# The expert layer joins the attention block: weights split on GpSimd beside the last heads, its layer norm by sequences, ranks made two tiles ahead

## The reference, cut to what matters

```python
x = x + _L0_attn_ref(_layernorm(x, axis=-1), ...)
x = x + _L0_ffn_ref(_layernorm(x, axis=-1), ...)
x = x + _L1_attn_ref(_layernorm(x, axis=-1), ...)     # 32 heads of 16, causal, ALiBi
x = x + _L1_ffn_ref(_layernorm(x, axis=-1), ...)      # below

scores = xf @ Wr.T                                    # 64 experts
top_vals, top_idx = jax.lax.top_k(scores, 16)
gates = jax.nn.softmax(top_vals, axis=-1)
G = zeros((N, 64)); G[n, top_idx] = gates
h = jnp.einsum('nd,krd->nkr', xf, A)                  # "ranks": 64 experts of rank 16
out = jnp.einsum('nkr,kdr->nd', h * G[:, :, None], B) * 2
```

## Time and profile before

| | us |
|---|---|
| median of 3 runs | 1530.74 (1530.06 to 1533.52) |
| the profiled execution, its own time | 1526.56 |
| its span, first to last instruction | 1524.8 |
| PE busy in the span | 1440.9 (94%) |
| DVE, ACT, POOL busy | 1020.6, 857.6, 537.7 |

### The profile page before, as it was taken

One profiled execution on the slowest core, in us unless ns is written; L12 is line 12 of the kernel. 1 busy time (PEld: TensorE's weight loads), 2 busy tenths in 40 slices (PEclk: granted clock), 3 DMA queues, 4 the chain that ended last, 5 costly groups with the idle time before them and its releaser, 6 DMA issues. The chain is left out here.

```text
span 1524.8 us, 25454 instructions
## 1 busy us (share of the span) xinstructions
PE 1440.9 (94%) x7696; PEld 1197.1 (79%) x7696; DVE 1020.6 (67%) x2549; ACT 857.6 (56%) x2184; POOL 537.7 (35%) x467
## 2 busy tenths in 40 slices
PE   6999999999999999999979999998799999985898
PEld 4788888888888888888867888887677777763687
DVE  7776667666677666776645333354788888997543
ACT  2766556665566655666543333212798989993110
POOL 5574465644656446563220000023433222101500
PEclk9999999999999999999999999999999999997999
DMA  5010010101101011000021111106445444403000
GB/s 169 10 47 15 28 43 21 34 14 27 41 21 34 14 27 41 21 14 8 8 84 42 63 61 42 55 0 110 98 77 105 77 103 78 84 1 114 8 21 28
DMA packets 37517, 71.98 MB, mean 47 GB/s; under 512 B 4992, under 2 KB 5376, under 8 KB 36864
## 3 DMA queue, kind: packets, MB, share of 16 engines
q1 hardware_dynamic: 29664, 55.35, 11.5%
q0 software_dynamic: 7776, 15.73, 7.2%
HBM read 60.58 MB, written 10.49 MB: 47 GB/s over the span
## 5 line engine op out<-in xcount | busy, mean ns | idle before, releaser
L822 ACT ACTIVATE a_probs<-a_probs,a_least 128x512 f32<-128x512 f32 (+3 forms) x256 | 143.0, 560 | 162.4 <-DVE a_least L683 157.7
L405 POOL TENSOR_TENSOR a_rotated<-a_by_cos,a_by_sin 128x512 f32<-128x512 f32 x80 | 103.7, 1296 | 223.8 <-DVE a_by_sin L706 221.7
L691 DVE TENSOR_TENSOR a_probsT_lo<-ps_out,a_probsT_hi 128x512 fp32r<-128x512 f32 (+3 forms) x256 | 118.6, 484 | 67.2 <-ACT a_probsT_hi L830 66.0
L830 ACT CAST a_probsT_hi<-ps_out 128x512 fp32r<-128x512 f32 (+3 forms) x256 | 101.5, 427 | 91.3 <-PE ps_out L556 90.5
L1774 ACT ACTIVATE a_probs<-a_probs,a_least 128x128 f32<-128x128 f32 (+3 forms) x256 | 142.1, 560 | 3.6 <-issue 1.8
L1658 DVE CUSTOM_DVE_ANT_0 a_probs<-ps_gate,a_causal 128x128 f32<-128x128 f32 (+3 forms) x256 | 117.1, 486 | 29.5 <-PE ps_gate L1508 19.4
L882 ACT ACTIVATE a_probs<-a_probs,a_inverse 128x128 f32<-128x128 f32 (+3 forms) x256 | 123.1, 553 | 9.6 <-DVE a_inverse L724 8.6
L64 PE MATMUL ps_up<-a_wo_hi,a_attended_hi 128*128 128x512 f32 x280 | 114.7, 410 | 6.6 <-DVE a_attended_lo L1738 1.7
L415 POOL TENSOR_TENSOR a_query_lo<-a_rotated,a_query_hi 128x512 fp32r<-128x512 f32 x64 | 82.6, 1291 | 107.6 <-ACT a_query_hi L842 107.6
L683 DVE CUSTOM_DVE_ANT_0 a_probs<-ps_out,a_causal 128x512 f32<-128x512 f32 (+2 forms) x192 | 101.1, 552 | 28.2 <-PE ps_out L66 28.1
L1666 DVE TENSOR_TENSOR a_probsT_lo<-ps_out,a_probsT_hi 128x384 fp32r<-128x384 f32 (+1 forms) x192 | 108.9, 596 | 2.6 <-ACT a_probsT_hi L1783 2.4
(11 more groups left out here) (271 smaller groups left out, 4083.3 us busy)
## 6 DMA issues: line engine op xcount, KB each, us to landing
a_raw<-in_wq SPq DMA_DIRECT2D x36, 256.0 KB, 2.7
a_raw<-in_wo SPq DMA_DIRECT2D x36, 256.0 KB, 2.7
a_stacked_q<-a_spill_q POOLq DMA_DIRECT2D x48, 128.0 KB, 4.6
a_stacked_k<-a_spill_k POOLq DMA_DIRECT2D x24, 256.0 KB, 4.3
f_raw<-in_gate SPq DMA_DIRECT2D x14, 256.0 KB, 2.8
f_raw<-in_up SPq DMA_DIRECT2D x14, 256.0 KB, 3.0
f_raw<-in_down SPq DMA_DIRECT2D x14, 256.0 KB, 3.6
a_raw<-in_wk SPq DMA_DIRECT2D x12, 256.0 KB, 2.8
```

Of the source, the lines that this page charges most:

```text
L405: nc.gpsimd.tensor_tensor(rotated[:], by_cos[:], by_sin[:], ALU.add).then_inc(rotation_added, 1)
L691: nc.vector.tensor_tensor(probsT[1][:, t % 2, 0:w], ps_turn[:, t % 2, 0:w], probsT[0][:, t % 2, 0:w].bitcast(F32), ALU.subtract).then_inc( ...
L822: nc.scalar.activation(tile, tile, ACT.Exp, bias=least[:, slot, i:i + 1], scale=-1.0, accum_out=total[:, slot, i:i + 1]).then_inc(exp_done, 1)
L830: nc.scalar.copy(probsT[0][:, t % 2, 0:w], ps_turn[:, t % 2, 0:w]).then_inc(turned_hi, 1)
```

## The change

`moe_phase` and its barrier are gone; a class `Moe` places the expert layer's tiles in memory that attention has done with, and the engines go on from the last head into it in the same block.

- **SP and GpSimd.** SP issues the loads of `down` and the router as soon as the last chunk's operands are out of their buffers. GpSimd splits them (18 instructions) behind its last attention piece, and then `up` (16 instructions) once all scores are made. ACT and DVE no longer split weights.
- **The order of the last outputs.** Tiles 0 and 1 are made in step 11 of the last chunk, tile 2 in step 12, tile 3 in step 13, and nothing in step 14. DVE takes each tile's moments right after adding it, and the layer norm of sequence 0 starts behind the last head. Tiles 4 to 7 are made later, between the router scores and the ranks of tile 0, in four different banks.
- **The layer norm by sequences.** Sequence 0 (tiles 0 to 3) comes first; sequence 1 follows between `rank(2)` and `rank(3)`. The router scores are made for half of the tokens at a time.
- **Ranks two tiles ahead.** PE's order is `turn(t + 1)`, `rank(t + 3)`, `make_out(t)`, so that what a tile's output needs is made one round before it. Outputs 5 and 7 have a bank of their own.

```diff
-SIDE1 = {0: "keys", 2: "values", 3: "spread", 4: "out", 6: "query"}
-BACK1 = (3, 5, 6)
+SIDE1 = {0: "keys", 2: "values", 3: "spread", 6: "query"}
+OUTS1 = {3: [(0, "back")], 4: [(1, "side")], 5: [(2, "back")], 6: [(3, "back")]}
+LAST_OUTS1 = {11: [(0, "back"), (1, "side")], 12: [(2, "side")], 13: [(3, "back")]}
...
     @block.sync
...
+        sp.wait_ge(query_out, 2 * 16 * 2 * CHUNKS1)
+        sp.wait_ge(keys_out, 2 * 16 * 2 * CHUNKS1)
+        moe.fetch_down(sp, (0, 1))
+        sp.wait_ge(side_made, side_count(CHUNKS1 - 1, 2))
+        moe.fetch_down(sp, (2, 3))
+        moe.sync(sp)
...
     @block.gpsimd
...
+        pool.wait_ge(score_made, 4 * (UNITS1 - HPC))
+        moe.split_first(pool)
+        pool.wait_ge(piece_split, piece_count(CHUNKS1 - 1, "wo"))
+        pool.wait_ge(score_made, 4 * UNITS1)
+        moe.split_up(pool)
...
     @block.tensor
...
+        moe.norm.turn(pe, 0)
+        turn_gathered(*last, *last)
+        moe.norm.ready(pe, 0)
+        pe.wait_ge(attend_read, UNITS1)
+        moe.make_scores(pe, 0)
+        turn_result(2 * CHUNKS1 - 1)
+        moe.rank(pe, 0, (0, 1))
+        moe.turn_scores(pe, 0)
+        for t in range(3):
+            make_last_out(t)
+        moe.rank(pe, 0, (2, 3))
+        make_last_out(3)
+        moe.tensor(pe)
...
     @block.vector
...
-                if last_steps:
+                if last_outs:
                     dve.wait_ge(read, count)
                     take_moments(nc, dve, m, 3, t)
...
+            if isinstance(c, int) and (c, s) == (CHUNKS1 - 1, STEPS1 - 2):
+                moe.norm.shift(dve, 0)
...
+        moe.norm.invert(dve, 0)
+        for t in range(QT):
+            moe.norm.normalise(dve, t)
+        for t in range(QT):
+            moe.norm.split(dve, t)
+        divide(*last)
+        split_attended(2 * CHUNKS1 - 1, CHUNKS1)
+        moe.pick(dve, 0)
+        for t in range(3):
+            add_last_out(t)
+        moe.gate_ranks(dve, 0)
+        add_last_out(3)
+        moe.vector(dve)
```

The new class, cut to the order of its work (its `pick`, `gate_ranks`, `turn` and `make_out` compute what those of `moe_phase` did; `pick` reads scores that ACT has copied out of PSUM for four tiles at once):

```diff
+    def split_first(self, pool):
...
+        def split(number, src, hi, lo, zero):
+            nc.gpsimd.tensor_tensor(hi, src, zero, ALU.add).then_inc(self.weights_hi, 1)
+            pool.wait_ge(self.weights_hi, number + 1)
+            nc.gpsimd.tensor_tensor(lo, src, hi.bitcast(F32), ALU.subtract).then_inc(self.weights_split, 1)
...
+    def sync(self, sp):
...
+        for i in range(2):
+            sp.wait_ge(self.weights_split, 4 * i + 5)
+            sp.dma_start(self.up_raw[i][:], m.dram["up1"][:, 4 * i:4 * i + 4, :]).then_inc(self.up_in[i], 16)
...
+    def tensor(self, pe):
+        every = range(DC)
+        self.rank(pe, 1, every)
+        self.turn(pe, 0)
+        self.rank(pe, 2, every)
+        pe.wait_ge(self.turned_split, 2)
+        self.norm.turn(pe, 1)
+        self.rank(pe, 3, every)
+        self.norm.ready(pe, 1)
+        self.turn(pe, 1)
+        self.make_out(pe, 0)
+        self.make_scores(pe, 1)
+        self.turn(pe, 2)
+        self.rank(pe, 4, every)
+        self.turn_scores(pe, 1)
+        self.make_out(pe, 1)
+        for t in range(2, NT):
+            if t + 1 < NT:
+                self.turn(pe, t + 1)
+            if t + 3 < NT:
+                self.rank(pe, t + 3, every)
+            self.make_out(pe, t)
...
+    def vector(self, dve):
+        norm = self.norm
+        norm.shift(dve, 1)
+        self.pick(dve, 1)
+        norm.invert(dve, 1)
+        for t in range(QT, NT):
+            norm.normalise(dve, t)
+        self.split_turned(dve, 0)
+        self.gate_ranks(dve, 1)
+        for t in range(QT, NT):
+            norm.split(dve, t)
+        self.pick(dve, 2)
+        self.gate_ranks(dve, 2)
```

More of the change, by code:

```diff
@@ L1219, in ffn0_attention1_phase, with outs @@
     result_turned, attended_split = sem("result_turned"), sem("attended_split")
-    def out_there(c, s):
-        return not isinstance(c, int) or (1 <= c if s < 8 else 0 <= c < CHUNKS1)
+    last_made, last_added = sem("last_made"), sem("last_added")
+    last = (CHUNKS1 - 1, STEPS1 - 1)
+    moe = Moe(nc, m, ctx, base, ffn, zeros, out)
+    def outs(c, s):
+        if not isinstance(c, int):
+            return OUTS1.get(s % 8, [])
+        if c == CHUNKS1 - 1 and s >= 8:
+            return LAST_OUTS1.get(s, [])
+        return OUTS1.get(s % 8, []) if (1 <= c if s < 8 else 0 <= c) else []
     def side(c, s):
@@ L1229, in side, with outs_until @@
             return what
[L1230 to L1240, removed]
+        return what if (c < CHUNKS1 - 1 if what == "query" or s >= 8 else 0 <= c < CHUNKS1) else None
     def steps_until(c, s):
-        steps = [(-1, k) for k in range(6, STEPS1)] + [(d, k) for d in range(CHUNKS1 + 1) for k in range(8 if d == CHUNKS1 else STEPS1)]
+        steps = [(-1, k) for k in range(6, STEPS1)] + [(d, k) for d in range(CHUNKS1) for k in range(STEPS1)]
         return [x for x in steps if x <= (c, s)]
+    def outs_until(c, s, bank):
+        return len([x for step in steps_until(c, s) for x in outs(*step) if x[1] == bank])
     def side_count(c, s):
@@ L1255, in back_count, with out_count @@
             return 6 * (c - 1) + back_count(1, s)
-        return len([x for x in steps_until(c, s) if back(*x)])
+        return outs_until(c, s, "back")
+    def out_count(c, s, at):
+        bank = outs(c, s)[at][1]
+        count = back_count(c, s) if bank == "back" else side_count(c, s)
+        return count - len([x for x in outs(c, s)[at + 1:] if x[1] == bank])
     def half_made(c, s):
@@ L1598, in step @@
                 norm.ready(pe, 1)
-            if s % 8 in (3, 4, 5, 6) and out_there(c, s):
-                make_out(c, s)
+            for at in range(len(outs(c, s))):
+                make_out(c, s, at)
             if side(c, s) in ("keys", "values", "query"):
@@ L1693, in step @@
                 divide(c2, s2)
[L1694 to L1699, removed]
+            for at, (t, to) in enumerate(outs(c1, s1)):
+                t += QT * (1 - s1 // 8)
+                bank, made, read = (ffn.ps_up[:, 1, :], back_made, back_read) if to == "back" else (ps_side, side_made, side_read)
+                count = out_count(c1, s1, at)
                 dve.wait_ge(made, count)
@@ L1817, in step @@
             if result_period(c1, s1) is not None:
[L1818 to L1821, removed]
+                round_attended(result_period(c1, s1), c1 + 1 if s1 >= 8 else c1)
+            if isinstance(c, int) and (c, s) == (CHUNKS1 - 1, STEPS1 - 2):
+                moe.norm.root(act, 0)
             if masked:
@@ L2076, in program @@
+        moe.norm.round(act, 0)
+        moe.copy_scoresT(act, 0)
+        round_attended(2 * CHUNKS1 - 1, CHUNKS1)
+        moe.copy_scores(act, 0)
+        moe.exponent(act, 0)
+        moe.scalar(act)
 def program(nc, dram, out):
```

485 lines of the change are left out of this document (252 added, 233 removed).

## The result

| | us |
|---|---|
| before, median of 4 runs | 1530.49 (1530.06 to 1533.52) |
| after, median of 4 runs | 1508.49 (1505.61 to 1514.89) |
| ratio, 95% interval | 0.9858 (0.9824 to 0.9892) |
| after, the profiled execution: time, span | 1514.89, 1512.8 |

What follows compares the result with a forecast made beforehand. Bound: the attention-to-expert seam, a chain through engines other than PE, then dense matmuls. Router start 1390.3 + clock 1.7 + dense work 106.9 = 1498.9 against 1521.5, 22.6 us less: median 1508.1 us, forecast 1505 to 1512 (0.66), range 1502 to 1517.

Steps and rivals of the forecast that it cites:

- Part 1, the last heads: DVE work put ahead of the last lo parts delays the last attend's end from 1379.4 to 1383.9, counting in full.
- Part 2, the layer norm: Sequence 0's normalisings, 4.9 us beside GpSimd's splits, then lo parts; router's matmuls start at 1390.3, 17.2 us earlier.
- Part 3, the clock: At the router's start, some nine matmuls run at half rate after PE's sparse work and wait: 1.7 us, or 0.
- The prediction's second case: Before the change, PE started at full rate after waiting 1.38 us behind dense matmuls; the slow case had waited 2.63 us.
- Part 4, dense to the end: From the router's start PE never waits for DVE's picks, gates and layer norm; costed at nothing beyond 106.9 us dense work.
- The slack: Between turned scores and gating of tile 1, DVE's chain leaves PE about 1.8 us to spare before `rank(3)`.
- an attention piece that is not moved: GpSimd's last attention piece, ending at 1348.9, after which the weight splits start; taken as unchanged.
- Less lost (B): GpSimd and DVE meet less often, or the clock stays up: 1503.8 us, or 1502.1 with the clock; chance 0.15.
- DVE holding PE in the middle (C): GpSimd still splits during sequence 1's picks and normalising, so PE waits: 8.5 us, 1516.6 us in all; chance 0.13.
- All of DVE held in the heads (D): Splits delay every mask and lo part in the heads, 4.5 us a step: 29 us lost, 1537 us; chance 0.04.
- Weights late (E): Splits of `down` end after `rank(0)` needs them at 1396, taking 2.8 us a split; no chance of its own.

Runs made afterwards that it cites:

- late_moments: Changed kernel with sequence 0's moments, variance shift and root moved behind the last head instead of inside the last steps: 1509.76 us, ratio 0.9855 to the kernel before.
- held_splits: Changed kernel with GpSimd's splits of `up` held until sequence 0's four tiles are normalised: 1507.83 us, ratio 0.9855 to the kernel before.

## Why the prediction held, point by point

**Part 1, the last heads.** 36.3 us forecast, 36.4 and 37.4 measured. The product took 1.43 us where the forecast had 0.8 more than free, the shift 0.37 where it had 0.7. Its 1.25 us from the last lo parts to the end of the attend is in no row: it is 1.50 before (1377.92 to 1379.42) and 1.47 after. Its reason "PE has nothing else to do, so it counts in full" was loose: late_moments shows that DVE's sum counts and not the attend's place.

**Part 2, the layer norm.** 4.9 us forecast for the normalisings, 5.43 and 5.44 measured; held_splits turned it into 1.92. GpSimd ended 45.6 us behind the split of `wo`, forecast 45.3. The Trainium skill's rule of the exclusive lock (page "SBUF — State Buffer", section "Who interferes with whom") agrees here on both sides: 1.43 us beside a split and 0.42 without for the product of two SBUF operands, while a pair of lo parts from PSUM took 1.27 us beside the splits and 1.29 behind them.

**Part 3, the clock.** 1.7 us or nothing. The two executions of the same kernel show both: matmuls 0.43 us apart and a mean granted clock of 0.79 in one, full rate in the other, 1.5 us apart in the last stage. A wait of 1.30 us stands ahead of both; which it will be can't be read from it. What came before differs: full clock under sparse work where the router then ran slow, a low stretch under the last heads where it ran at full rate. The prediction's second case is like the latter: the nine dense matmuls ahead of the 1.38 us wait ran at a granted clock of 0.50 (1386.16 to 1390.37 in before), which it did not say. But this makes no rule: held_splits has the full clock on both sides of its wait of 1.61 us, late_moments a low one on both sides of 0.55 us. Of the ten profiles of changed kernels two start the router slowly, the first and late_moments.

**Part 4, dense to the end.** Right: no wait. A tile takes 11.8 us, not 11.94 (transposes of ranks at 1456.17, 1467.97 and 1479.75 in the chain below): 8 x 0.15 = 1.2 us less, about the 1.0 us by which the last stage lies under the forecast. So the prediction's "no other order of the same matmuls can make it shorter" is not quite right: the 24 matmuls of a tile's output took 5.60 us in before (1460.36 to 1465.96) and 5.44 after (1462.37 to 1467.81), at the same granted clock of 1.00. Why is open. The slack was also less than the 1.8 us that it gave, and ran out earlier than at `rank(3)`: where one pick lost 2.3 us (held_splits), PE waited 0.99 us ahead of the layer norm's transposes of sequence 1, which leaves some 1.3 us there (an estimate from these two).

```profile
1456.17 0.87 PE ps_out L1285 x8
...
1467.97 0.88 PE ps_out L1285 x8
...
1479.75 0.87 PE ps_out L1285 x8
```

**The step that failed** is one that the prediction did not write down. It costed the load of `up` and let GpSimd's start hang "on an attention piece that is not moved". That piece moved: the loads of `down` and of the router, 2.2 MB, were put beside the last read-back of keys, and the heads lost 4.6 and 5.3 us (33.7 and 34.3 against 29.0): a wait of 2.8 and 3.8 us for the slope rows, and 5 to 6 us at about half the granted clock behind it. With the loads made to wait, both are gone. The forecast for the stages behind the piece is 151.3 us, measured 150.5 and 149.0. In the sum the trace gives 18.7 and 19.6 us won in place of 22.6; the medians have 22.0 and, in the repetition, 20.8. The forecast median of 1508.1 so rests in part on luck. Executions of one kernel lie up to 9 us apart, and the profiled one of before was 3.9 us quicker than its median; that the rest lies in stages ahead of the change is argued from this, not shown.

**The rivals.** Less lost (B): not in the changed kernel; it is what held_splits makes. DVE holding PE in the middle (C): 0, and 1.0 us where the splits were moved onto the pick. All of DVE held in the heads (D): only the products, about 1 us each when they meet a split, and the shift. Weights late (E): not; made late on purpose they cost 7.4 us.

## What to carry to other kernels

Early work for a later stage is free only where neither its instructions nor its transfers stand beside something that waits: ask of each load that moves up which transfers are under way then and who waits for them, and let it wait for them if it has time to spare. When a helper engine's work is put beside a busy one, place it instruction by instruction: the same 16 splits of `up` cost VectorE 3.5 us beside four normalisings, 2.3 beside one pick, and nothing beside work that reads PSUM. And measure a stage from a landmark that both kernels share: differences of 2 us stood clearly in the stages and not in the medians.

## What the runs showed of the hardware

- Beside GpSimd's splits, DVE instructions on SBUF differ: `moe_chosen`, `moe_gated` and `moe_gates` took 0.63, 1.36 and 0.98 us against 0.20, 0.22 and 0.25, while `MATCH_REPLACE8` stayed at 0.21, in both. Being all-SBUF alone does not make an instruction wait.
- The same 1.30 us wait of PE was followed by a granted clock of 0.50 (1401.92 to 1405.00) in one execution and by 1.00 in another of the same program, whose low stretch (0.59 over 8.3 us) lay ahead of it.
- A wait of 2.79 us in the middle of the heads, entered at a granted clock of 1.00, was followed by 6.4 us at 0.53; one of 3.81 us by 5.4 us at 0.51.
- Loads on SP's queue slowed small ones on GpSimd's: with four loads of 512 KB beside them, the slope rows of 256 KB took 11.8 and 12.5 us to land, and 5.4 and 5.6 without.
